# One turn of TensorE in a graph attention kernel: where the first half of the key fold is issued

## What is computed

```python
h = relu(layernorm(x))                                  # the x of what follows
e = leaky_relu(h @ a[:256] + (h @ a[256:]).T, 0.2)
U = softmax(where(adj > 0, e, -9e15), axis=1)           # 8192 x 8192
rowsum = sum(U * 0.5 * U, axis=1)
feat = shrink(combination of h, U @ h and h * rowsum)   # shrink by 1e-6
out = x + combination of feat, U @ feat, feat * rowsum and h0
```

## Time and profile before

| | |
|---|---|
| median of 3 runs | 1397.99 us |
| the profiled execution | 1395.99 us, span 1394.4 us |
| TensorE busy | 912.4 us, 65% of the span |
| VectorE busy | 933.2 us, 67% |
| ScalarE busy | 861.5 us, 62% |
| GpSimd busy | 588.4 us, 42% |
| granted TensorE clock, mean | 0.843 of full speed |
| stage: loop turns of the first pass | 311 to 983 us, 51 turns |

### The profile page before, as it was taken

How to read it: one execution, slowest core, us unless ns; L and a number is a source line. 1 busy time by engine, 2 the same in 40 slices (tenths; PEclk the granted TensorE clock), 3 DMA queues, 4 the chain that set the end, 5 groups by cost and what they waited for, 6 DMA issues and landing times.

```text
span 1394.4 us, 27679 instructions
## 1 busy us (share of the span) xinstructions
PE 912.4 (65%) x3566; PEld 561.5 (40%) x3630; DVE 933.2 (67%) x5233; ACT 861.5 (62%) x1840; POOL 588.4 (42%) x649
## 2 busy tenths in 40 slices
PE   3555657777766666667767767777556556566665
PEld 2431145444344433334333434433335444454443
DVE  7765736668888888888888888888782223334444
ACT  4675467778988888888888888888524222111111
POOL 2014325344433233322212222222376777777775
PEclk9985678889998999999888887878757777889899
DMA  6988796789999999999999999999236656777886
GB/s 174 354 321 294 275 382 250 296 320 384 395 388 375 373 384 379 394 380 380 389 381 363 380 381 366 382 379 363 70 93 191 177 173 181 213 224 227 249 260 199
DMA packets 152837, 423.14 MB, mean 303 GB/s; under 512 B 31111, under 2 KB 114697, under 8 KB 136406
## 3 DMA queue, kind: packets, MB, share of 16 engines
q1 hardware_dynamic: 122492, 345.66, 66.3%
q0 software_dynamic: 30304, 77.05, 18.2%
HBM read 398.37 MB, written 33.90 MB: 310 GB/s over the span
## 4 chain that ended last, share of the span: by engine, by line
DVE 28%; issue 24%; PE 16%; DMA 14%; POOL 6%; ACT 5%; DVEq 3%; POOLq 2%; ACTq 2%; SPq 0%
PE ACC L689 5%; DMA W<-feat_d,IDT 4%; POOL W L634 4%; PE TP L321 3%; DMA R<-sc_d 3%; DVE XHO L1061 2%; PE MISC L982 2%; DMA R<-in_x_dram 2%; PE ACC L693 1%; POOLq L623 1%; POOL R L634 1%; DMA pt_d<-R 1%; ACT SG L309 1%; DMA R<-haug_d 1%; DVE RE L1193 1%
## 5 line engine op out<-in xcount | busy, mean ns | idle before, releaser
L309 ACT ACTIVATE SG<-W,ABOVE 128x4096 bf16<-128x4096 f32 x126 | 467.0, 3706 | 58.7 <-DVE cnt L1044 47.0
L634 POOL DMA_INDIRECT R<-haug_d,IDS x230 | 230.4, 1002 | 583.0 <-issue 563.0
L321 PE MATMUL TP<-SG,FOLD 128*128 128x512 bf16 x948 | 280.5, 435 | 4.5 <-issue 0.6
L680 ACT ACTIVATE DG<-ident,WSR 128x128 f32<-128x128 f32 x230 | 75.7, 391 | 268.6 <-PE ACC L694 254.0
L1747 DVE SCALAR_TENSOR_TENSOR R<-ACC,SELF,R 128x256 f32<-128x256 f32 x63 | 30.5, 484 | 214.3 <-PE ACC L694 214.0
L688 PE MATMUL ACC<-XHO,ZB 128*128 128x256 bf16 x126 | 39.5, 314 | 196.0 <-DMA W<-feat_d,IDT 97.1
L321 PEld LDWEIGHTS TP<-SG,FOLD 128*128 128x128 bf16 x1008 | 111.8, 119 | 110.6 <-issue 47.7
L689 PE MATMUL ACC<-R,DG 128*128 128x256 f32 x446 | 153.9, 494 | 0.0
L634 POOL DMA_INDIRECT W<-feat_d,IDR x140 | 133.8, 956 | 42.6 <-issue 40.5
L689 PEld LDWEIGHTS ACC<-R,DG 128*128 128x128 f32 x446 | 100.7, 242 | 16.9
L688 PEld LDWEIGHTS ACC<-XHO,ZB 128*128 128x128 bf16 x126 | 12.4, 98 | 226.0 <-DMA W<-feat_d,IDT 115.6
(11 more groups left out here) (295 smaller groups left out, 2250.4 us busy)
## 6 DMA issues: line engine op xcount, KB each, us to landing
W<-in_adj_dram SPq DMA_DIRECT2D x128, 2048.0 KB, 10.2
haug_d<-R POOLq DMA_DIRECT2D x8, 1056.0 KB, 9.7
HTS<-haug_d SPq DMA_DIRECT2D x64, 132.0 KB, 10.0
R<-in_x_dram SPq DMA_DIRECT2D x8, 1024.0 KB, 6.6
R<-in_x_dram SPq DMA_DIRECT2D x64, 128.0 KB
R<-in_L_gnn_h_dram SPq DMA_DIRECT2D x64, 128.0 KB
R<-feat_d SPq DMA_DIRECT2D x64, 128.0 KB
out_dram<-R SPq DMA_DIRECT2D x64, 128.0 KB, 2.0
```

What stands on the lines that cost most here:

```text
L309: nc.scalar.activation(SG[:, u, half(h)], W2[:, u, half(h)], ACT.Sign, scale=2.0 ** 100, bias=ABOVE[:], accum_out=DEG[:, u, h:h + 1]).then ...
L321: nc.tensor.matmul(KP[u], FOLD[:, b], SG[:, u, b * FW:(b + 1) * FW], start=False, stop=False)
L634: pool.indirect_dma_start(out=g[:, k, 0:w], out_offset=None, in_=table, in_offset=bass.IndirectOffsetOnAxis(ap=ids[:, k:k + 1], axis=0), * ...
L680: nc.scalar.mul(DG[:, u, k], ident[:], weights[:, k:k + 1])
```

## The change

The first quarter of the fold for tile t+2 (L317 and four L321) is issued behind SPW and ahead of the first slot products. The second quarter (four L321) is issued between the arrival sums and the edge spread, where the first quarter was. Behind the edge spread no fold is left. Nothing is added or removed, and only TensorE's order changes.

```diff
@@ first_tensor, body @@
                     nc.tensor.matmul(SPW, RE[:, ub], WS[:, ub, 0:K], start=True, stop=True).then_inc(w_spread, 1)
                     slots = slots_of(pe, tb + 1)
+                if live(-2):
+                    fold(pe, t + 2, q + 1, u, 0, NB // 4)
+                if live(2):
                     pe.wait_ge(diag_begun, tb + 1)
                     first_products(pe, slots, ub, G[:, ub])
                 if live(0):
...
                     nc.tensor.matmul(SUMS[:, KC:2 * KC], TRI[:], RC[:], start=True, stop=True).then_inc(sums_made, 1)
                     if live(-2):
-                        fold(pe, t + 2, q + 1, u, 0, NB // 4)
+                        fold(pe, t + 2, q + 1, u, NB // 4, NB // 2)
                     pe.wait_ge(edges_ready, t + 1)
                     nc.tensor.matmul(SPR, RE[:, u], ED[:], start=True, stop=True).then_inc(spread, 1)
-                    if live(-2):
-                        fold(pe, t + 2, q + 1, u, NB // 4, NB // 2)
                 if blocks == 2:
                     extra0(2 * t - 3, q, u)
```

## The result

The changed kernel takes 1402.85 us, the median of 6 runs (1401.31 to 1403.69); the kernel before, in 6 runs beside it, 1396.53 us (1394.73 to 1400.0). The ratio is 1.0038, 95% interval 1.0022 to 1.0055. The change makes the kernel slower by about 0.4%: inside the range I gave at the end (1388 to 1406), outside the forecast's own 1391 to 1400, with the sign opposite to the small gain I forecast. The step that failed is the loss term, 14 turns at 0.4 us = 5.6 us for the low clock over the start of the turn: it came to 30 turns and 16.2 us.

The account below looks back on a forecast made before the run. VectorE was taken to set the pace. Terms -5.5 - 3 + 5.6 = -2.9 us against the profiled 1396.0 gave 1393.1; that execution being 2.0 us below the median, forecast 1395, own range 1391 to 1400, widened to 1388 to 1406.

Parts of the forecast that it names:

- What bounds the kernel: Loop turns: VectorE sets the pace; TensorE lengthens one only by late arrival sums, edge spread or spread of the weights.
- The upper bound of a gain: VectorE's waits at L1182 and L1199: 6.5 and 5.3 us can be won, together 11.8 us, 0.8% of the time.
- The first quarter ahead of the products costs nothing: Ahead of the slot products: 1.23 us of matmuls fit 1.23 us of idle time; bounds 0 and 0.9 us a turn.
- The second quarter ahead of the edge spread costs nothing: Between arrival sums and edge spread: 0.85 us of matmuls where 1.23 us were; gain in time nearly nothing, 0.
- The clock's gain: Slot products and edge spread run less at the low clock: 5.5 us won at sums, 3 at spread, -8.5 us.
- The clock's loss: Low clock over the turn's start makes L1148 wait 0.4 us in 14 of 40 later turns: 5.6 us, ends 0 and 24.
- the signs: Wrong if L1148 waits in nearly all later turns or none, or L688's products start late at low clock, delaying sums.
- my upper bound of 0.6: At L1148: the wait per late turn runs from nothing to 1.9 + 0.8 - 2.07 = 0.6 us.
- my own slower rival: Low clock at the start of most of 40 later turns, L1148 waits 0.5 us each: +11.5 us, 1409 us, chance 0.14.
- Nothing behind the edge spread: End of turn: other_products and transpose come 0.85 us earlier, which in later turns is only more idle time; 0.
- The head: Five turns where ScalarE waits 17.1 us for a store: that covers the sums, counted 0; ends -7.2 and +4.5 us.

Follow-up runs that it names:

- the fastest order: Against the change: second quarter back behind the edge spread, twelve extra unread matmuls between arrival sums and edge spread; 1382.7 us, ratio 0.9905 to the kernel before.
- the first quarter alone: Against the kernel before: only the first quarter moved ahead of the slot products, the second kept behind the edge spread; 1395.3 us, ratio 0.9987.

## Why the prediction went wrong, by its steps

**What bounds the kernel**: right. VectorE sets the turn, and the loops differ by how late TensorE is for VectorE. I named three places; L1069, which reads the moved scores, is a fourth. In the change it costs 1.1 us, with extra matmuls at the end of the turn up to 5.7.

**The upper bound of a gain**, 6.5 + 5.3 = 11.8 us: right. In the fastest order the sums gained 6.5 us and the edge spread 5.2; the loop is 12.4 us shorter in all, and no order tried went below 658.8 us.

**The first quarter ahead of the products costs nothing**: right at the full clock, shown by the first quarter alone and by the same place filled with extra matmuls. **The second quarter ahead of the edge spread costs nothing**: right in the change. With both quarters there the wait at that place is up to 2.0 us, so the cover is thin.

**The clock's gain**, -8.5 us: there, and larger. The sums gave 6.4 us, where I took 5.5, and the edge spread 4.9, where I took 3: -11.4 us. Of the 6.4 us only 4.2 came in the first 11 turns, and those turns won just 149.0 - 148.5 = 0.5 us in all, where I had put 0.5 us on each: five of them are late at L1149, for which I had counted none of the 11.

**The clock's loss**, 14 turns at 0.4 us = 5.6 us: this step failed. The mechanism, its place and the line are as forecast, and none of the signs came by which I had said I would be wrong. But 30 turns are late at L1149, not 14, and by 0.54 us each, not 0.4: 16.2 us. Of the 30, 25 are among the 40 later turns. With the gain, the moved scores and the rest, -11.4 + 16.2 + 1.1 - 0.5 = +5.4 us. Both factors were too small; in 17 of the 30 the price was 0.63 us or more, past my upper bound of 0.6, as both stretches from MOV to the spread ran low and not the fold's alone. That the kernel lost no more is partly luck: the gain was 2.9 us above what I took. The count was a choice without a row behind it. What speaks for a high count stood in my own slower rival: a turn with the wait meets the next low stretch at the same place. The slow turns do come in runs: after L1149's first waits in every other turn there are eight in a row from 419 to 527 us. Why a run goes on, because the low level returns after 13.6 us and the turn after 13.55, is argued from the stretches above and not shown, and so is why it ends; no run here set it apart. Nor is it shown why the low level lasts 6.2 us on average in the change and 4.4 before.

**Nothing behind the edge spread**, "only more idle time": true and not harmless. With eight extra matmuls in that idle time VectorE no longer waits for the next turn's spread of the weights. I had tied it to the end of the turn, and the same eight between sums and spread do as much.

**The head**: right, 0. **The tail** I had left out: its first turn lost 1.2 us.

The Trainium skill names a remedy for its own case in "TensorE: Matmul & The Clock Gate", section "HAM oscillation — how this bites in real kernels": restructure the loop, or pad the matmuls, so that TensorE stays at its full clock. The runs agree with the aim, by a means of their own: with the first quarter moved, 12 small matmuls a turn whose results nobody reads take 0.95% off the kernel, and the move alone 0.13%. The same section's price, half of the time at the lower level, does not carry over. The change's loop has a mean clock of 0.81:

```profile
311.00:988.00 677.00, 524.14 (x2045) 286.00 (x2044) 562.97 (x3470) 572.43 (x1173) 197.85 (x199) 0.81 0.97 374
```

That is 0.38 of 677 us at the lower level, by the page's price an estimate of 129 us. The loop at 1.00, with the second quarter behind the edge spread and 12 extra matmuls, is 676.8 - 659.0 = 17.8 us shorter: VectorE sets the pace and most of the slow work is covered.

## To carry to other kernels

Where the clock of TensorE falls in most turns of a loop, moving matmuls into an idle gap can move the low stretch too: look where the idle time goes, and what stands on the path in the stretch behind it. If an engine other than TensorE sets the pace, a few unread matmuls in an idle gap can be worth more than the order of the real ones, and they must not stand ahead of what that engine waits for. Price a late instruction from start to start, not by the idle time alone. A count of turns in a sum needs a row behind it, or else both ends of the range must carry its whole span.

## What was not expected of the hardware

Extra work made the kernel faster by its place: eight matmuls of 128 x 256 (twelve take 1.47 us at the full clock) in each turn shortened the change's loop by 18.0 us between sums and edge spread, and by 10.8 us at the end of the turn. The level fell without a long idle gap: 41 times in the change's 51 turns, in which TensorE's longest gap is 1.69 us; one of the stretches ahead of a fall is shown above, with TensorE busy for 1.40 of 3.40 us. And one of the chips took 1530 us for the kernel that takes 1396 on the others; for the fastest order the loop took 680.4 us there (from 314.9 to 995.3) against 659.0, and what lies behind the loop 1524.1 - 995.3 = 528.8 us against 1380.1 - 966.7 = 413.4.
